# Preparing attention's first batch and weights inside the last Mamba body, in a decoder layer on one core

## What is computed

```python
x = x + mamba(layernorm(x))              # in_proj, conv of 4, silu, scan over 16 states, out_proj
x = x + cross_attention(layernorm(x), ctx)
x = x + experts(layernorm(x))            # 8 experts, top 2, capacity 1.2

def cross_attention(q, c):               # 16 heads of 32
    qh = (q @ Wq.T + bq); kh = (c @ Wk.T + bk); vh = (c @ Wv.T + bv)
    probs = softmax(qh @ kh.T / sqrt(32))
    return (probs @ vh) @ Wo.T + bo
```

## Time and profile before

| | |
|---|---|
| median of 3 runs | 2726.71 us (2725.51 to 2731.23) |
| the profiled execution | 2724.42 us, its span 2722.8 us |
| PE busy | 2476.7 us, 91% of the span |
| DVE, ACT, POOL busy | 1543.5, 1216.4, 648.0 us |
| DMA | 254.73 MB, mean 94 GB/s |
| mean granted PE clock | 0.947 of full speed |

### The profile page before, as it was taken

How to read it: one execution, slowest core, us unless ns; L and a number is a source line. 1 busy time by engine, 2 the same in 40 slices (tenths; PEclk the granted TensorE clock), 3 DMA queues, 4 the chain that set the end, 5 groups by cost and what they waited for, 6 DMA issues and landing times. The chain is left out here.

```text
span 2722.8 us, 48116 instructions
## 1 busy us (share of the span) xinstructions
PE 2476.7 (91%) x17244; PEld 2187.9 (80%) x17245; DVE 1543.5 (57%) x2560; ACT 1216.4 (45%) x1911; POOL 648.0 (24%) x1040
## 2 busy tenths in 40 slices
PE   5999999999995699999999996269999999999997
PEld 4999999999994578787877874258888888888886
DVE  5788788788884255666665654733443334433332
ACT  6565565555561244444444442024443444434442
POOL 2111111111111344444444431120311203113011
PEclk9999999999997699999999997579999999999999
DMA  3100100100102566666666651321524415234131
GB/s 111 34 33 25 47 25 24 47 25 24 48 18 75 139 163 171 174 174 171 178 171 174 171 151 41 98 69 62 135 76 121 104 62 135 78 119 104 63 81 19
DMA packets 232739, 254.73 MB, mean 94 GB/s; under 512 B 68264, under 2 KB 158376, under 8 KB 232464
## 3 DMA queue, kind: packets, MB, share of 16 engines
q1 hardware_dynamic: 191504, 231.17, 28.9%
q0 software_dynamic: 40960, 20.41, 4.3%
HBM read 182.47 MB, written 68.80 MB: 92 GB/s over the span
## 5 line engine op out<-in xcount | busy, mean ns | idle before, releaser
L2100 DVE TENSOR_TENSOR d_h_l<-d_hf,d_h_h 128x616 fp32r<-128x616 f32 x124 | 99.2, 800 | 395.4 <-ACT d_h_h L1926 395.4
L320 PE MATMUL a_psP<-a_xnT_h,a_win_l 128*128 128x256 f32 x1024 | 304.8, 298 | 16.8 <-ACT a_zs L554 10.0
L1839 PE MATMUL d_psH<-d_xgT_h,d_w_l 128*128 128x308 f32 x1024 | 315.7, 308 | 3.5 <-ACT d_hf L1962 2.1
L1840 PE MATMUL d_psH<-d_xgT_l,d_w_h 128*128 128x308 f32 x1024 | 312.8, 305 | 0.0
L1841 PE MATMUL d_psH<-d_xgT_h,d_w_h 128*128 128x308 f32 x1024 | 312.5, 305 | 0.0
L1962 ACT ACTIVATE d_hf<-d_psH,d_b1c 128x308 f32<-128x308 f32 x256 | 130.9, 518 | 384.5 <-PE d_psH L1841 384.5
L321 PE MATMUL a_psP<-a_xnT_l,a_win_h 128*128 128x256 f32 x1024 | 295.5, 289 | 0.0
L322 PE MATMUL a_psP<-a_xnT_h,a_win_h 128*128 128x256 f32 x1024 | 294.9, 288 | 0.0
L1803 POOL DMA_INDIRECT out_dram<-d_ob,d_to x40 | 103.7, 2592 | 686.4 <-ACT d_ob L1979 676.0
L1839 PE MATMUL d_psO<-d_w_h,d_h_l 128*123 128x512 f32 x620 | 244.2, 394 | 0.0
L1841 PE MATMUL d_psO<-d_w_h,d_h_h 128*123 128x512 f32 x620 | 244.0, 394 | 0.0
(11 more groups left out here) (325 smaller groups left out, 6219.6 us busy)
## 6 DMA issues: line engine op xcount, KB each, us to landing
d_w<-in_W_dram SPq DMA_DIRECT2D x64, 1024.0 KB, 6.1
b_qst<-qs_d SPq DMA_DIRECT2D x48, 512.0 KB, 6.6
b_kst<-ks_d SPq DMA_DIRECT2D x48, 512.0 KB, 6.6
a_xl<-in_x_dram SPq DMA_DIRECT2D x16, 512.0 KB, 4.2
a_xres<-in_x_dram SPq DMA_DIRECT2D x16, 512.0 KB, 3.7
x_d<-a_xres SPq DMA_DIRECT2D x16, 512.0 KB, 3.1
b_xa<-x_d SPq DMA_DIRECT2D x16, 512.0 KB, 9.4
b_cx<-in_ctxT_dram SPq DMA_DIRECT2D x16, 512.0 KB, 10.1
```

The source lines that it names most:

```text
L320: pe.matmul(out, lo_w, hi_x, start=first, stop=False)
L1839: pe.matmul(out, lo_w, hi_x, start=first, stop=False)
L1840: pe.matmul(out, hi_w, lo_x, start=False, stop=False)
L2100: dve.tensor_tensor(out, a, b_, ALU.subtract).then_inc(done, 1)
```

## The change

The two stages now share tiles (class Shared): the weights w_h and w_l, which held Mamba's input weights, xnT, the split context c_h and c_l (Mamba's xproj weights), raw (Mamba's xl), xres, and stage (Mamba's xc of even batches). Mamba's body 15 normalises and turns attention's batch 0 as if it were a batch 16, and its last body splits it, loads and splits the context and the four halves of Wq and Wk, and starts the two halves of Wv. In attention body 0 every q or k tile has a PSUM bank and a slot (in PT) of its own. In Mamba the flags are fetched ahead of the store of x1 and of the load of xres, and in the last body they are reduced ahead of add_res. Batch 1 is normalised within body 0 of attention, its rsqrt after the fourth tile.

```diff
 # Mamba, SP
             def body(b, par, prev, cur):
+                sp.wait_ge(ln, 7 * b + 7)
+                if isinstance(b, int) and b == B - 1:
+                    sp.wait_ge(x1_st, 16)
+                    sp.dma_start(xl, x1_v[0]).then_inc(x_ld, 16)
+                elif cur:
+                    sp.dma_start(xl, x_v[b + 1]).then_inc(x_ld, 16)
+                else:
+                    sp.dma_start(sh.raw[:].rearrange("p (k s) -> p k s", k=KD), ctxT[0].rearrange("(k p) s -> p k s", p=P)).then_inc(sh.cx_ld, 16)
+                    sp.wait_ge(y2_rdy, 8 * (B - 1))
+                    sp.wait_ge(t1_ok, 8 * (B - 1))
+                    for c in range(2):
+                        sp.dma_start(sh.stage[:, c, :], weight(c)).then_inc(sh.w_ld[c], 16)
...
-                    wait(sp, x1_st, 16 * (b - 1))
+                    if not cur:
+                        with nc.allow_non_contiguous_dma(reason="small parameters"):
+                            for to, src in small:
+                                sp.dma_start(to, src).then_inc(sh.p_ld, 16)
+                        next_weight(2)
+                    if not (isinstance(b, int) and b == 1):
+                        sp.wait_ge(res, 2 * (b - 1))
+                        sp.dma_start(x1_v[b - 2], xres[:]).then_inc(x1_st, 16)
+                        sp.wait_ge(x1_st, 16 * (b - 1))
                     sp.dma_start(xres[:], x_v[b - 1]).then_inc(xres_ld, 16)
-                    sp.wait_ge(res, 2 * b)
-                    sp.dma_start(x1_v[b - 1], xres[:]).then_inc(x1_st, 16)
-            run(body, sp, lambda: sp.wait_ge(x1_st, 16 * B))
+                    if not cur:
+                        for c in range(3, 6):
+                            next_weight(c)
+            def next_weight(c):
+                sp.wait_ge(sh.w_hi, c - 1)
+                sp.wait_ge(sh.w_lo, c - 1)
+                sp.dma_start(sh.stage[:, c % 2, :], weight(c)).then_inc(sh.w_ld[c % 2], 16)
+            def tail():
+                sp.wait_ge(res, 2 * B)
+                sp.dma_start(x1_v[B - 1], xres[:]).then_inc(x1_st, 16)
 # Mamba, POOL, after the last body's t1_ok
+                    pool.wait_ge(sh.cx_ld, 16)
+                    for k in range(KD):
+                        g.tensor_copy(sh.c_h[:, c], sh.raw[:, c]).then_inc(sh.cx_hi, 1)
+                        g.tensor_tensor(sh.c_l[:, c], sh.raw[:, c], f32(sh.c_h[:, c]), ALU.subtract).then_inc(sh.cx_lo, 1)
 # Mamba, ACT, last body
                 if prev and not cur:
+                    next_hi(0)
                     mt_hi_()
+                    next_hi(1)
                 for d in range(KE):
+                    if not cur and d in (2, 4):
+                        next_hi(1 + d // 2)
 # Mamba, DVE
                 if prev:
+                    if not cur:
+                        next_lo(0)
                     dve.wait_ge(m_mm, b)
...
+                    if not cur:
+                        flags(b)
                     if not (isinstance(b, int) and b == 1):
                         add_res(b - 2)
...
                         y2_(d)
+                        if not cur and d in (0, 2, 4):
+                            next_lo(1 + d // 2)
 # attention
+        t8_h, t8_l = (PT[:, i].rearrange("p g t s -> p (g t) s").bitcast(F32R) for i in range(2))
+        banks = [psQ[:, 0:S], psV[:, 0:S]] + [t[:, g, :] for t in (psT, *psS) for g in (0, 2)]
...
                 def qk_tile(i):
-                    if i:
+                    ps = banks[i] if first(b) else psQ[:, 0:S]
+                    if i and not first(b):
                         pe.wait_ge(qk_f, U * b + i)
...
                 for i in range(U):
                     if cur:
                         qk_parts(i)
-                    if cur and i < KD:
+                    if cur and i < KD and not first(b):
                         cx_part(i)
+                    if first(b) and i == 3:
+                        rsqrt(b, ln, ve, rs, rstd)
```

More of the change, by code:

```diff
@@ L474, in mt_hi_, with next_hi @@
                     copy(MT_h[:], MTf[:], mt_hi)
+                def next_hi(c):
+                    act.wait_ge(sh.w_ld[c % 2], 16 * (c // 2 + 1))
+                    copy(sh.part(sh.w_h, c), sh.stage[:, c % 2, :], sh.w_hi)
+                wait(act, z_mm, 8 * b)
+                for h in range(2):
+                    act.wait_ge(xn_tp, 2 * b + h + 1)
+                    copy(xnT_h[:, 2 * h:2 * h + 2, :], psT[h][:].rearrange("p (k s) -> p k s", k=2), xnT_hi)
                 if cur:
[L478 to L481, removed]
                     if isinstance(b, int) and b == 0:
@@ L746, in xt_lo_ @@
                     minus(XT_l[:, :, c], psT[j % 2][:].rearrange("p (t s) -> p t s", t=TT), f32(XT_h[:, :, c]), xt_lo)
-                more = cur and not (isinstance(b, int) and b == B - 1)
                 for d in range(KE):
@@ L856, in attention_phase @@
         ctx_v = ctxT.rearrange("b (k p) s -> b p k s", p=P)
-        stage = [V[i] for i in range(2)]
-        weights = (WqT, WkT, WvT, WoT)
+        banks = [psQ[:, 0:S], psV[:, 0:S]] + [t[:, g, :] for t in (psT, *psS) for g in (0, 2)]
         def run(body, eng, written_out=False):
@@ L878, in run, with v_bank, tile @@
             body(B + 1, 1, False, False, True)
+        def v_bank(b, t):
+            return psV if first(b) and t else psQ
+        def tile(b, i):
+            hi, lo, n = (t8_h, t8_l, i) if first(b) else (t_h, t_l, i % 2)
+            return hi[:, n, :], lo[:, n, :]
         def last(b):
@@ L909, in store @@
                         sp.wait_ge(qk_lo, U * b + first + i + 1)
-                        for part, t in enumerate((t_h, t_l)):
-                            sp.dma_start(f32(scratch[part, i * P:(i + 1) * P, :]), f32(t[:, (first + i) % 2, :])).then_inc(st_[i % 2], 16)
+                        for part in range(2):
+                            sp.dma_start(f32(scratch[part, i * P:(i + 1) * P, :]), f32(tile(b, first + i)[part])).then_inc(st_[i % 2], 16)
                 def load(scratch, st_, ld, stack, parts):
@@ L926, in body @@
                     sp.dma_start(xres[:], x1_v[b - 2]).then_inc(xres_ld, 16)
-                if cur and not last(b):
-                    sp.wait_ge(ln, 7 * b + 7)
+                if cur and not last(b) and not first(b):
+                    sp.wait_ge(ln, 7 * b)
                     sp.dma_start(xa[:], x1_v[b + 1]).then_inc(xa_ld, 16)
@@ L1035, in body @@
                         rsqrt(b - 2, ln3, ve3, rs3, rstd3)
-                if cur and not last(b):
-                    rsqrt(b + 1, ln, ve, rs, rstd)
+                if cur and not last(b) and not first(b):
+                    rsqrt(b, ln, ve, rs, rstd)
             run(body, pool)
@@ L1050, in turn_xn @@
                 pe.wait_ge(ln, 7 * b + 7)
-                if not first(b):
-                    wait(pe, exp_s, U * (b - 2) + 6)
+                if first(b):
+                    pe.wait_ge(qk_f, 4)
+                wait(pe, exp_s, U * (b - 1) + 6)
                 for kk in range(KD):
@@ L1258, in body @@
                     v_tile(1)
-                if cur and not last(b):
-                    turn_xn(b + 1)
+                if cur and not last(b) and not first(b):
+                    turn_xn(b)
                 if prev:
@@ L1382, in body @@
                     v_copy(1)
-                if cur and not last(b):
-                    split_xn(b + 1)
+                if cur and not last(b) and not first(b):
+                    split_xn(b)
                 if prev:
@@ L1465, in body @@
                 if first(b):
-                    for c in range(2, 8):
+                    for c in range(4, 6):
                         weights_lo(c)
@@ L1518, in body @@
                 if more:
-                    dve.wait_ge(xn_tp, b + 1)
-                    normalize(b + 1, ln, xa, mv, rs, rstd, xn)
-                    split_xn(b + 1)
+                    wait(dve, xn_tp, b)
+                    normalize(b, ln, xa, mv, rs, rstd, xn)
+                    if first(b):
+                        for c in range(6, 8):
+                            weights_lo(c)
+                    split_xn(b)
                 if prev:
```

215 lines of the change are left out of this document (119 added, 96 removed).

## The result

The changed kernel takes 2681.9 us (median of 4 runs, 2674.5 to 2684.7) against 2727.8 us for the kernel before beside it: a ratio of 0.984, with a 95% interval of 0.9825 to 0.9854, so 40 to 48 us faster. The forecast was 2685.6 in a range of 2678 to 2696. The profiled execution took 2681.22 us, with a span of 2679.5 (2722.8 before: 43.3 less) and a mean clock of PE of 0.954 (0.947).

The account below looks back on a forecast made before the run. It took PE, busy 91% of the span, as the bound, with a dip from Mamba to attention. Terms -1.5, -41.1 and +1.5 sum to -41.1 us: 2683.3 for the profiled execution, 2685.6 us against the median, range 2678 to 2696.

Parts of the forecast that it names:

- Steady bodies, -1.5: Steady Mamba bodies: fetching flags ahead of the store saves 1.5 us in all, between 0 and 3.
- Body 15, 0: Mamba's body 15: normalising one batch more adds no time, its flag still taken at 828.21.
- MT_l, +2.4: Last Mamba body: waiting for the first weight half ends MT_l at 835.3 instead of 832.85, costing 2.4 us.
- The ports, +1: Last Mamba body: three DVE operations on PE's path meet POOL's casts at shared ports, costing 1 us, 0 to 3.
- The loop, "which PE sets": Last Mamba body's loop: PE sets its pace, so the third and fourth weight halves are hidden, otherwise 1.2 us each.
- Covered, with 1 to 2 us to spare: Mamba's last loop: the fourth weight half, issued near 842, arrives before ACT wants it near 848.
- the hand-over loses: Rival, Mamba to attention: late weight halves and port meetings cost 5 to 9 us, giving 2691 to 2695; chance 0.22.
- The hand-over, -2.4: Mamba to attention: SP's 2.4 us wait for the last store goes, so attention opens at 860.1.
- POOL's path and the queue: Attention's first body: POOL, then SP's queue, set the pace; q stack 34.7 us earlier, scores 41.1 us earlier at 903.0.
- Given back, +1.5: Start of body 1's scores: PE runs at half clock after idling, costing 1.5 us, 1 to 2.5.
- Half the gain only: Rival, attention body 2: body 1's chain for q of batch 1 takes back 20 us, giving 2706; chance 0.04.
- slower: Rival, Mamba bodies: xres loaded too late costs 14 bodies from 3.3 us each, 2733 with 3.4; chance 0.02.

Follow-up runs that it names:

- e_cast: The changed kernel with POOL's two long casts into the k stacks moved behind the eight splits of attention's first body; 2680.0 us.
- e_onebank: The changed kernel with all eight q and k tiles of attention's first body in one PSUM bank again, the eight slots kept; 2684.2 us.
- e_slots: The changed kernel with its eight banks but only two slots for the split tiles in attention's first body; 2687.8 us.
- e1_flags: The flags alone: the kernel before with only the flags loaded ahead of the x1 store and reduced right behind MT_l in the last Mamba body; 2714.8 us.
- e1_gb: The kernel before with the flags part alone, plus the scan's result gb sharing its buffer with l_r; 2712.3 us.
- e_mt: The changed kernel with the last Mamba body's first weight half split behind MT_l and the flags, not ahead of MTf; 2688.3 us.
- e_best: The changed kernel with long casts behind the splits, context and bias loads behind the k stack, DVE's weight halves later in Mamba's last body; 2678.7 us.
- e_late: The changed kernel with POOL's split of the first context moved from the last Mamba body back to attention's opening, behind its casts; 2687.1 us.
- e_queue: The changed kernel with the next context and output bias loads issued behind the k stack in attention's first body; 2679.8 us.

## Why the prediction was right, step by step

The forecast was 3.7 us above the measured median. In the profile it had 41.1 us, and 43.3 were measured: 40.7 up to the experts' first transfer, and 2.6 in the experts, which it did not reckon. That its own part comes out within 0.4 us is luck in some measure, since several of the terms below are off and cancel.

- **Steady bodies, -1.5.** The part alone gave 2.4; in the changed kernel they gave nothing (706.7 and 706.2 us for 14, where it was 706.0). DVE's 9.7 us of waits are gone, as said. What the step lacked was what stood under the wait: a fall of the clock in most bodies. And the changed kernel's bodies are 0.2 us longer than those of the flags alone, at a full clock (49.8 against 49.6) and at a fall (50.6 against 50.4). The shared gb is not the cause; the waits of PE and the lengths of the instructions in the two traces agree, and the cause is open. Other tiles that now lie elsewhere are one candidate, which was not tried.
- **Body 15, 0.** The flag is written at 829.53 and not at 828.21, 1.3 us late, though the work of this body was reckoned rightly. Stretches at the start of body 15, columns as in the earlier trace rows, in the kernel before, the changed one and e_cast:

```profile
781.60:789.60 8.00, 7.96 (x65) 7.54 (x65) 6.24 (x13) 4.16 (x9) 1.04 (x2) 1.00 0.22 72
...
781.70:789.70 8.00, 8.00 (x55) 7.96 (x55) 5.49 (x11) 3.32 (x8) 0.74 (x1) 0.79 0.20 72
...
782.70:790.70 8.00, 7.97 (x65) 7.60 (x65) 6.25 (x13) 4.18 (x9) 1.06 (x2) 1.00 0.21 76
```

  From this body's MTf to its flag it is 45.65 us before and 46.81 in the changed kernel, in whose trace the clock falls. In the three kernels with the extra batch and without a fall (e_cast, e_onebank, e_slots) it is 45.8; in e1_flags and e1_gb, with a fall and without the extra batch, 46.6. So the extra batch costs 0.1 us and the fall 1.0.
- **MT_l, +2.4.** It ends at 836.1, forecast 835.3. The sum was near, its make-up not: the flag is 1.3 later, PE's M comes later behind it (MTf 3.8 us behind the flag in e_mt, 2.9 before; eight transposes more stand ahead, but e1_flags, without them, has 3.4), and the weight half costs 1.1, as e_mt shows, not 2.4.
- **Flags and y2.** Reduced at 836.05 (835.3), then y2 after 2.73 us, as before. The second half ahead of y_l: from y2 to the output projection 2.35 us instead of 1.45, so 0.9 where 1.2 was reckoned.
- **The ports, +1.** Misplaced. POOL's split ran from 853.5 to 858.6, when the loop was nearly over, since POOL stood at issue for 15.8 us ahead of it, through its branches for the eight tiles; it met two DVE operations, for some tenths each. That such meetings cost what was said stands, by e_mt and by DVE's 8.24 us. No split stands beside the three DVE operations ahead of the output projection for which the 1 us was reckoned.
- **The loop, "which PE sets".** Not by PE alone. It took 16.6 us, where the forecast kept the 15.9 of before. In e_cast, e_slots and e_onebank the clock is at 1.00 when it starts, and it takes 16.5, 16.9 and 19.6; in six others, e_mt and e_best left out, it starts at 0.50 and takes 16.1 to 17.9. DVE's y2 also needs POOL's answer for each tile: in e1_flags it waits 0.4 to 1.0 us for POOL's program in six of the eight tiles.
- **"Covered, with 1 to 2 us to spare", the fourth half.** True of four traces, the changed kernel's among them, and not of six with the same order there, in which ACT waited 0.2 to 1.8 us for it: the store ahead lands in 3.4 to 5.0 us. This is the part of the rival "the hand-over loses" that does come true in some executions.
- **The hand-over, -2.4.** From PE's last matmul to the opening 2.2 us instead of 4.6: exact. The opening at 860.3, forecast 860.1.
- **POOL's path and the queue.** The fourth tile split at 876.4 (876.3), the q stack at 878.7 (878.6), the k stack at 892.9 (893.3), the scores at 902.4 (903.0): the two terms that carry nine tenths of the gain hold within 0.7 us, and e_late and e_queue confirm their prices where these are changed alone (4.2 us for four pairs of POOL's, 4.6 by the forecast; 2.1 us for 768 KB). The steady bodies' 1.5 us are not in these forecast times; with them the scores were due at 901.5.
- **Given back, +1.5.** The cause is there: from the scores on, the clock is 0.50 over 2.6 us and 0.67 over the next 3.0, where it was 0.80 and 1.00, an estimate from these of 1.8 us. The q stack of batch 1 is 41.0 us earlier and the experts' first transfer 40.7, so 1.0 less than the scores. As this stretch scatters by 7.8 us between the traces, that these traces differ by no more is luck.
- **Not reckoned, -2.6**, in a stage that the diff does not touch (below).

"Half the gain only" and "slower" did not come near: behind body 1 the k stacks are issued 45 to 47 us apart, as before.

Three of the signs that were named would have misled. "A Mamba body longer than 49.5 us" was true of the kernel before (50.1 to 50.5). "ACT stands for weights within the loop" came true in six traces and cost little. And attention's first matmuls did not run without a gap: PE stood 6.56 us until 878.66, which cost nothing, as it later stood 12.65 us for the k stack.

## What to carry to other kernels

Where a stage opens with an empty pipeline, price each engine's instructions and the queue's bytes in series and see which comes last; what the change removed elsewhere (a bank here, the longest wait of the profile here) may be worth nothing. A wait that is taken away from a full engine gives only the part under which nothing else lay, and a fall of the clock may lie there. Before moving work into another stage's loop, look at what it sits beside: a small instruction of POOL's behind a long one of DVE's lasts as long as that one.

## What was not expected of the hardware

The experts' stage is shorter, by 2.9 us on average, in all eleven traces made from the changed kernel (1022.0 to 1024.1 us from its first transfer to the end) than in the three made from the one before (1025.3 to 1026.0). Most of it, 2.4 us, sits at one instruction, POOL's first gather. DVE's ids and that gather, in the kernel before:

```profile
1777.45 0.16 DVE L2124 TENSOR_TENSOR d_ids<-d_num,d_psT 123x5 int32<-123x5 f32 x1
...
1781.24 1.78 POOL L1786 DMA_INDIRECT d_xg<-xn_d,d_ids  x1 [66.40 <-issue]
```

And in the changed kernel:

```profile
1737.11 0.16 DVE L2223 TENSOR_TENSOR d_ids<-d_num,d_psT 123x5 int32<-123x5 f32 x1
...
1738.50 1.78 POOL L1885 DMA_INDIRECT d_xg<-xn_d,d_ids  x1 [64.34 <-issue]
```

3.8 us from the ids to the gather there, 1.4 here. In the two other traces made from the kernel before it is 3.6 and 3.8, and in all eleven made from the changed one 1.4; the program of POOL is the same at this place and only what stands ahead of it differs. The profile calls the time "issue", but its DMA queues show more. Between the ids and the gather, in the kernel before:

```profile
q14 instruction: 1, 0.01, 0.5%
```

One packet of the DMA queue whose kind the profile calls "instruction" falls between the two in each of the three traces made from the kernel before, and none in any of the eleven others. So POOL most likely waits for its program to be loaded there, at a place that moves with the length of the code ahead; no edit has tried it. The row does not say which engine the packet is for.

The other surprise is the clock: it falls in steady bodies with PE fully busy (0.79 over 8 us, as if 3.4 of them were at half), the body is 0.8 to 0.9 us longer for it, and when the same kernel is traced again other bodies are hit.
